# Four engines in one Mamba unit: gate and product for u later in the scan order, GpSimd's drives first, a tanh in PSUM, epsilon as a column of a product

## The chip, the cores and the metric

One core of one Trainium2 chip. The metric is the device time of one execution in microseconds (us), lower is better; a kernel's figure is the median of its runs. TensorE does the products, VectorE the scans and elementwise work that reads PSUM, ScalarE the activations, GpSimd elementwise work on SBUF, SyncE issues DMAs. In profile rows they are PE (PEld for its weight loads), DVE, ACT, POOL and SP.

## The reference

Six blocks in a row on a batch of two images of 16 x 16 positions and 64 channels: triangular edge attention, attention with rotary embedding, attention with 8 heads of 64, a top-2 mixture of 8 experts, a stack of six Mamba layers and a second mixture of experts, with normalisations and residuals. The change concerns the Mamba stack alone:

```python
for i in range(6):
    residual = hidden if residual is None else hidden + residual
    h = residual * rsqrt(mean(residual ** 2) + 1e-5) * norm_w[i]
    u, z = split(h @ in_w[i])                       # 128 channels each, 256 positions
    uc = silu(causal_conv(u, cw[i]) + cb[i])        # 4 taps
    dt_r, Bm, Cm = split(uc @ xp_w[i])              # 16, 16, 16
    dt = softplus(dt_r @ dt_w[i] + dt_b[i])
    s = exp(dt[..., None] * A) * s + (dt * uc)[..., None] * Bm      # scanned over 256 positions
    y = sum(s * Cm) + uc * Dp
    hidden = (y * silu(z)) @ out_w[i]
```

## The kernel before, in words

The kernel is written by hand, engine by engine: each engine's block is a fixed list of instructions in program order, and semaphores alone tie the engines together. No scheduler reorders anything: what stands behind a waiting instruction on its engine waits too.

The Mamba stack is 12 **units**, u = 2 * layer + image (`UNITS`). A unit holds channels on 128 partitions and 256 positions (N) along the free axis; its 16 states are four groups g = 0 to 3 of four (`SG`), so one scan runs over 4 x 256 = 1024 columns. The two images alternate, so that unit u+1 is prepared while u is scanned; unit u+1 of the same image as u-1 needs u-1's output. In one turn of the loop over u:

- **VectorE**: `prep_dt(u)` (three products on 256 columns: L1151 finishes the softplus polynomial, L1154 makes `dt`, L1157 makes `dtu` = dt * uc), `drive(u,0)` (L1170, dtu times the spread B of group 0), `gate(u-1)` (L1163, y of the unit before times its gz), four `scan`s (L1179), `drive(u,1)`, `prep_uc(u+1)` (L1145) and `weigh_last` (L1189, group 3 times C in two halves).
- **GpSimd**: `drive(u,2)` and `drive(u,3)` (L1689), `prep_rms(u+1)` (L1672 adds epsilon, L1674 takes the power -0.5), six halves of `weigh` for groups 0 to 2 (L1700, scanned states times C, 512 columns each) and `prep_gz` (L1680, z times its sigmoid).
- **ScalarE**: sixteen `decay`s (L1484, exp(dt * A) into PSUM, four per scan; `da` has two buffers, so those of group g+2 wait for scan g), and u+1's preparation: square and sum (`prep_norm`, L1414), scaling (`prep_hs`, L1428), `ht` (L1434), tanh for silu(u) (`prep_tu`, L1440), the copy of z (`prep_zs`, L1445), `xds` and `stack` (L1458, L1459), the softplus steps (L1468 to L1474), and z's sigmoid (L1451, L1453).
- **TensorE**: `out_proj(u-1)` after the gate (L708, L711, its sum with the residual stays in PSUM as `hidp`), the spreads of B and C (`replicate`, L664), for u+1 the transposes, the convolution (`prep_in`, L633 to L635), z's product (L640) and `prep_x`, and `sum_y` (L698): sixteen products with the identity that add up y, each when its piece of `hc` is there. The last one raises `m_y`.
- **SyncE** stores `xds` and reads it back spread over all partitions: groups 2 and 3 of B, 0 to 2 of C, five loads of 512 KB per unit.

The chain from one unit to the unit after next runs through all engines: gate(u-1), out_proj(u-1), prep_norm(u+1), GpSimd's prep_rms(u+1), prep_hs, transposes, ht, prep_in, tu, prep_uc(u+1), prep_x, softplus, prep_dt(u+1). The order that matters most here is GpSimd's:

```python
for u in range(UNITS):                   # GpSimd, before
    drive(u, 2)
    if u and more: prep_rms(u + 1)
    weigh(u, 0, 2)
    drive(u, 3)
    weigh(u, 1, 2); weigh(u, 2, 2)
    if more: prep_gz(u + 1)
```

## Time and profile before

| what | value |
|---|---|
| time, median of 3 runs | 377.95 us (376.48 to 378.31) |
| the profiled execution's own time | 374.24 us |
| its span, first to last instruction | 372.4 us |
| busy: PE, DVE, ACT, POOL | 88%, 78%, 63%, 54% |
| mean granted TensorE clock | 0.945 |
| the Mamba loop, first scan to last scan's start | 159.6 to 339.3 us |

The span is cut on the page into 40 slices of 9.3 us; the Mamba loop fills slices 18 to 37, where DVE's digit is 9 throughout. Busy shares over the whole span mix six blocks; the loop has to be read by itself, in order of time. A row of a timeline has start, duration, engine, line, operation, tiles and count; a bracket is idle time of the engine before it and what ended it. Instructions of one engine may overlap by some 0.08 us, so costs below are taken from start to start.

### The profile page before, as it was taken

To read this page: it belongs to the slowest core of one execution; us is meant where nothing else is said; L and a number is where in the kernel's file an instruction comes from. 1 tells how busy PE (TensorE), PEld (TensorE's weight loads), DVE (VectorE), ACT (ScalarE), POOL (GpSimd) and SP (SyncE) were. 2 spreads that over 40 slices of the span, in tenths; PEclk is the share of its full clock that TensorE was granted. 3 is DMA by queue.
4 is the path that set the end of the run, shared out by engine and by line. 5 is a ranking of instruction groups with operands and counts; after the bars stand their busy time and mean duration, and the time that the engine had idled before them with its cause. 6 is when DMAs were issued, how large, how long until landed. Compare 5 with 4: busy or idle time off the path is not lost.

```text
span 372.4 us, 5741 instructions
## 1 busy us (share of the span) xinstructions
PE 327.1 (88%) x1904; PEld 230.4 (62%) x1904; DVE 289.1 (78%) x496; ACT 235.7 (63%) x674; POOL 199.3 (54%) x199
## 2 busy tenths in 40 slices
PE   4866999899999999869999999999999999978684
PEld 3354776556557646647677676676766767656462
DVE  2674476888794626199999999999999999999463
ACT  1102348888792563777877878778787787873163
POOL 2879300000000140188978989798897988979000
PEclk9995589999999699999999999999999999998978
DMA  7960400000000030257173471734518246260000
GB/s 214 373 125 2 128 2 1 2 0 3 3 0 2 0 114 2 73 213 250 54 267 121 163 236 52 282 114 172 217 73 282 95 191 197 92 282 0 3 0 14
DMA packets 19751, 41.07 MB, mean 110 GB/s; under 512 B 7986, under 2 KB 10626, under 8 KB 19594
## 3 DMA queue, kind: packets, MB, share of 16 engines
q1 hardware_dynamic: 19434, 40.38, 31.8%
q8 instruction: 15, 0.25, 0.3%
q10 hardware_dynamic: 288, 0.33, 0.3%
q14 instruction: 14, 0.11, 0.1%
HBM read 40.31 MB, written 0.39 MB: 109 GB/s over the span
## 4 chain that ended last, share of the span: by engine, by line
PE 40%; DVE 33%; ACT 14%; POOL 5%; issue 5%; DMA 1%; POOLq 0%; DVEq 0%; SPq 0%; ACTq 0%
DVE big L1179 15%; ACT PS L1484 7%; POOL big L1700 4%; PE PS L521 4%; DVE big L1189 3%; DVE big L1151 3%; PE PS L698 3%; PE PS L297 2%; PE PS L485 2%; PE PS L640 2%; PE PS L415 2%; PE PS L585 2%; PE PS L291 2%; PE PS L495 2%; DVE unit_t L1154 1%
## 5 line engine op out<-in xcount | busy, mean ns | idle before, releaser
L1179 DVE TENSOR_TENSOR_SCAN big<-PS,big 128x1024 f32<-128x1024 f32 x48 | 109.5, 2285 | 3.0 <-ACT PS L1484 2.5
L698 PE MATMUL PS<-big,cst 128*128 128x256 f32 x384 | 98.2, 393 | 5.5 <-POOL big L1700 4.5
L1484 ACT ACTIVATE PS<-unit_t,amat 128x255 f32<-128x255 f32 x192 | 82.5, 467 | 21.3 <-DVE unit_t L1154 18.1
L1700 POOL TENSOR_TENSOR big<-big 128x512 f32<-128x512 f32 x72 | 89.4, 1268 | 2.4 <-DVE big L1179 2.2
L698 PEld LDWEIGHTS PS<-big,cst 128*128 128x128 f32 x384 | 68.2, 192 | 25.3 <-POOL big L1700 17.1
L1689 POOL TENSOR_TENSOR big<-unit_t,big 128x1024 f32<-128x1024 f32 x24 | 57.4, 2390 | 15.8 <-DMA big<-spill 15.8
L1656 POOL TENSOR_TENSOR w2t<-w2t,w0t 128x768 f32<-128x768 f32 x2 | 3.6, 1812 | 88.8 <-DVE big L1113 88.8
L1295 ACT ACTIVATE big<-PS 128x512 f32<-128x512 f32 (+1 forms) x43 | 24.7, 583 | 22.6 <-PE PS L521 7.4
L1347 ACT ACTIVATE big<-PS,big 128x256 f32<-128x256 f32 x64 | 29.6, 473 | 1.8 <-DVE big L953 1.7
L1170 DVE TENSOR_TENSOR big<-unit_t,PS 128x1024 f32<-128x1024 f32 x24 | 29.0, 1208 | 1.3
L953 DVE TENSOR_REDUCE big<-PS 128x2 f32<-128x512 f32 x32 | 22.0, 688 | 6.6 <-PE PS L415 3.2
L521 PE MATMUL PS<-cst,big 128*128 128x128 f32 x128 | 20.9, 285 | 3.2 <-ACT big L1295 1.9
L664 PE MATMUL PS<-stack,pick_b 96*128 96x256 bf16 x144 | 22.1, 276 | 1.2 <-DVE big L1170 1.2
L521 PEld LDWEIGHTS PS<-cst,big 128*128 128x128 f32 x128 | 13.5, 140 | 14.4 <-DVE big L962 6.9
L962 DVE TENSOR_SCALAR big<-big 128x256 f32<-128x256 f32 x64 | 19.7, 350 | 1.1
L664 PEld LDWEIGHTS PS<-stack,pick_b 96*128 96x128 bf16 x144 | 14.1, 99 | 7.9 <-DVE big L1170 1.6
L297 PE MATMUL PS<-cst 128*128 128x256 f32 x52 | 15.8, 442 | 0.3 <-ACT wdt L1295 0.3
L1189 DVE TENSOR_TENSOR big<-big,PS 128x512 f32<-128x512 f32 x24 | 15.4, 684 | 0.4
L1151 DVE SCALAR_TENSOR_TENSOR big<-big 128x256 f32<-128x256 f32 x12 | 10.2, 854 | 5.2 <-ACT big L1474 5.2
L1672 POOL TENSOR_TENSOR msq<-ssq,eps_t 128x2 f32<-128x2 f32 x11 | 2.1, 194 | 20.8 <-ACT sqs L1414 20.8
L1347 ACT ACTIVATION_READ_ACCUMULATOR big<-PS,big 128x1 f32 x64 | 13.2, 207 | 0.0
L1464 ACT ACTIVATE stack<-PS 96x256 bf16<-96x256 f32 x24 | 8.9, 370 | 6.2 <-PE PS L656 6.2
...
## 6 DMA issues: line engine op xcount, KB each, us to landing
...
```

Source lines behind the costliest of these rows:

```text
L297: pe.matmul(PS[:, bank, N:2 * N], ident, CONST.of(cst, "rope")[:, 0:N], start=True, stop=True)
L521: last = pe.transpose(PS[:, 6 + t, m * N + a * P:m * N + (a + 1) * P], probs[:, i % SLOTS, a, m * P:(m + 1) * P], ident)
L664: last = pe.matmul(PS[:, 4 + c, s * N:(s + 1) * N], pick_b[:, col:col + 1].to_broadcast([96, P]), stack[u % 2][:], start=True, stop=True)
L698: last = pe.matmul(yps, ident, hc[:, g, s], start=False, stop=True, skip_group_check=True)
L1170: v.tensor_tensor(dbu[:, g], dtu[u % 2].unsqueeze(1).to_broadcast([P, SG, N]), BCv, ALU.mult)\
L1179: v.tensor_tensor_scan(flat(hst[:, g]), flat(da[g % 2]), flat(dbu[:, g]), 0.0, ALU.mult, ALU.add).then_inc(sem("m_h"), 1)
L1189: v.tensor_tensor(hc[:, g, s], hst[:, g, s], BCv[:, s], ALU.mult).then_inc(sem("m_hc3"), 1)
L1295: copy = lambda dst, src, **kw: act.activation(dst, src, ACT.Copy, **kw)
L1347: act.activation(probs[:, i % SLOTS, a], PS[:, i % 4, a * N:(a + 1) * N], ACT.Exp, bias=rowmax[:, i, a:a + 1], accum_out=rowsum[:, i, a:a ...
L1484: one = act.activation(da[g % 2][:, n, 1:N], dt[u % 2][:, 1:N], ACT.Exp, scale=amat[:, u // 2, col:col + 1])
L1689: pool.tensor_tensor(dbu[:, g], dtu[b].unsqueeze(1).to_broadcast([P, SG, N]), bsp[b][:, SG * (g - 2):SG * (g - 1)], ALU.mult).then_inc(sem ...
L1700: pool.tensor_tensor(hc[:, g, s:s + size], hst[:, g, s:s + size], csp[u % 2][:, SG * g + s:SG * g + s + size], ALU.mult).then_inc(sem("m_h ...
```

## The change: what it does

In the turn of the loop for unit u:

1. **VectorE**: `gate(u-1)` moves behind `scan(u,0)`, `prep_uc(u+1)` from behind scan 1 to behind scan 2.
2. **GpSimd**: `prep_gz(u-1)` (it was gz of u+1 at the turn's end) and both drives come first, then the six halves of `weigh` in the order of `weigh_order`. `prep_rms` keeps its place behind the first drive.
3. **ScalarE**: all of group 1's decays and two of group 2's come ahead of `prep_norm`; z is copied and its sigmoid made in unit u itself, not a unit ahead; the softplus takes its exponential first, and its last tanh is written into PSUM (`outer`, free columns of `da[0]`), where L1151 (now L1156) reads it.
4. **TensorE**: the second spread comes first, then `out_proj`; z's product comes behind it, `sum_y` follows `weigh_order`.
5. **Epsilon**: a matmul adds a column sqrt(64 * 1e-5) to each half of `hidp`, ScalarE squares and sums 65 columns, and GpSimd's addition (L1672) goes, but for u = 1.

```diff
 VectorE
             v.wait_ge(sem("m_sp"), 4 * u + 4)
-            v.scalar_tensor_tensor(sp_l, sp_w, LOG_D / LOG_S, sp_u, ALU.add, ALU.mult)...
+            v.scalar_tensor_tensor(by_four(sp_l), outer, LOG_D / LOG_S, by_four(sp_u), ALU.add, ALU.mult)...
...
             for u in range(UNITS):
                 prep_dt(u)
                 drive(u, 0)
+                scan(u, 0)
                 if u:
                     gate(u - 1)
-                scan(u, 0)
                 drive(u, 1)
                 scan(u, 1)
+                scan(u, 2)
                 if u + 1 < UNITS:
                     prep_uc(u + 1)
-                scan(u, 2)
                 scan(u, 3)
                 weigh_last(u)
 GpSimd (prep_rms)
                 pool.wait_ge(sem("m_ssq"), u)
-                pool.tensor_tensor(msq[b][:], ssq[b][:], eps_t[:].to_broadcast([P, 2]), ALU.add)...
-                pool.wait_ge(sem("m_rms"), 2 * u - 1)
-                pool.tensor_tensor(rms[b][:], msq[b][:], power_t[:].to_broadcast([P, 2]), ALU.pow)...
+                mean = ssq[b]
+                if u == 1:
...
+                pool.tensor_tensor(rms[b][:], mean[:], power_t[:].to_broadcast([P, 2]), ALU.pow)...
 GpSimd (loop)
+        weigh_order = [(0, 0), (1, 0), (2, 0), (1, 1), (0, 1), (2, 1)]
             for u in range(UNITS):
+                if u:
+                    prep_gz(u - 1)
                 drive(u, 2)
-                if u and more:
+                if u and u + 1 < UNITS:
                     prep_rms(u + 1)
-                weigh(u, 0, 2)
                 drive(u, 3)
-                weigh(u, 1, 2)
-                weigh(u, 2, 2)
-                if more:
-                    prep_gz(u + 1)
+                for g, h in weigh_order:
+                    weigh(u, g, h)
+            prep_gz(UNITS - 1)
 ScalarE (prep_softplus, then the loop)
+                act.activation(sp_u, sp_a, ACT.Exp, scale=-1.0, bias=logs_t)...
+                act.activation(sp_v, sp_a, ACT.Tanh, scale=LOG_K, bias=turn_t)...
                 prep_part(u, 1)
-                act.activation(sp_w, sp_v, ACT.Tanh, scale=LOG_M, bias=shift_t)...
+                act.activation(outer, by_four(sp_v), ACT.Tanh, scale=LOG_M, bias=shift_t)...
+                prep_part(u, 2)
...
                 decay(u, 0, every)
-                decay(u, 1, every[0:2])
+                decay(u, 1, every)
+                decay(u, 2, every[0:2])
                 if u and more: prep_norm(u + 1)
+                prep_zs(u)
                 if u: keep_residual(u - 1)
-                decay(u, 1, every[2:3])
+                decay(u, 2, every[2:3])
                 if u and more: prep_hs(u + 1)
-                decay(u, 1, every[3:4])
-                decay(u, 2, every[0:1])
+                prep_zt(u)
+                decay(u, 2, every[3:4])
                 if more: prep_ht(u + 1)
-                decay(u, 2, every[1:4])
+                decay(u, 3, every[0:3])
                 if more: prep_tu(u + 1)
...
+                prep_zc(u)
                 decay(u, 3, every[3:4])
                 if more: prep_softplus(u + 1)
 TensorE
+                spread_second(u)
                 if u:
                     out_proj(u - 1)
+                prep_in_z(u)
+                spread_last(u)
...
+                sum_y(u, 3, (1, 2))
+                sum_y(u, 0, (2, 3))
+                sum_y(u, 1, (3,))
+                sum_y(u, 3, (3,))
+                sum_y(u, 2, (2, 3)).then_inc(sem("m_y"), 1)
```

GpSimd, one turn of the loop for an odd unit. `ssq` and `rms` carry the image's number; unit_t holds uc, gz, dt, dtu, z, and big the drives, states and weighed states. Before:

```order
L1689 TENSOR_TENSOR big<-unit_t,big 128x1024 [waits m_h,m_dtu,ld_B12]
L1672 TENSOR_TENSOR msq0<-ssq0,eps_t 128x2 [waits m_ssq]
L1674 TENSOR_TENSOR rms0<-msq0,power_t 128x2 [waits m_rms]
L1700 TENSOR_TENSOR big<-big 128x512 [waits m_y,m_h,ld_C10]
L1700 TENSOR_TENSOR big<-big 128x512
L1689 TENSOR_TENSOR big<-unit_t,big 128x1024 [waits m_h,m_dtu,ld_B13]
L1700 TENSOR_TENSOR big<-big 128x512 [waits m_y,m_h,ld_C11]
L1700 TENSOR_TENSOR big<-big 128x512
L1700 TENSOR_TENSOR big<-big 128x512 [waits m_y,m_h,ld_C12]
L1700 TENSOR_TENSOR big<-big 128x512
L1680 TENSOR_TENSOR unit_t<-unit_t 128x256 [waits m_zt]
```

The same turn in the changed kernel:

```order
L1684 TENSOR_TENSOR unit_t<-unit_t 128x256 [waits m_zt]
L1693 TENSOR_TENSOR big<-unit_t,big 128x1024 [waits m_h,m_dtu,ld_B12]
L1678 TENSOR_TENSOR rms0<-ssq0,power_t 128x2 [waits m_ssq]
L1693 TENSOR_TENSOR big<-unit_t,big 128x1024 [waits m_h,m_dtu,ld_B13]
L1703 TENSOR_TENSOR big<-big 128x512 [waits m_y,m_h,ld_C10]
L1703 TENSOR_TENSOR big<-big 128x512 [waits m_y,m_h,ld_C11]
L1703 TENSOR_TENSOR big<-big 128x512 [waits m_y,m_h,ld_C12]
L1703 TENSOR_TENSOR big<-big 128x512 [waits m_y,m_h,ld_C11]
L1703 TENSOR_TENSOR big<-big 128x512 [waits m_y,m_h,ld_C10]
L1703 TENSOR_TENSOR big<-big 128x512 [waits m_y,m_h,ld_C12]
```

Behind the power of `ssq` stand the same drive and six weighs as before, with the drive now ahead of the first two weighs and without the addition ahead of the power; gz, of the unit before, has moved from the end to the head of the turn.

VectorE, from `prep_dt(u)` to the last scan, in the same turn. Before:

```order
L1151 SCALAR_TENSOR_TENSOR big<-big 128x256 [waits m_sp]
L1154 SCALAR_TENSOR_TENSOR unit_t<-PS,big 128x256 [waits m_xs,m_poly]
L1157 SCALAR_TENSOR_TENSOR unit_t<-unit_t 128x256 [waits m_uc,m_dt]
L1170 TENSOR_TENSOR big<-unit_t,PS 128x1024 [waits m_dtu,m_BC]
L1163 TENSOR_TENSOR unit_t<-PS,unit_t 128x256 [waits m_gz,m_y]
L1179 SCALAR_TENSOR_TENSOR big<-PS,big 128x1024 [waits m_hc,m_da,m_dbu]
L1170 TENSOR_TENSOR big<-unit_t,PS 128x1024 [waits m_BC]
L1179 SCALAR_TENSOR_TENSOR big<-PS,big 128x1024 [waits m_hc,m_da,m_dbu]
L1145 SCALAR_TENSOR_TENSOR unit_t<-unit_t,PS 128x256 [waits m_tu]
L1179 SCALAR_TENSOR_TENSOR big<-PS,big 128x1024 [waits m_hc,m_da,m_dbu_pool]
L1179 SCALAR_TENSOR_TENSOR big<-PS,big 128x1024 [waits m_da,m_dbu_pool]
```

In the changed kernel:

```order
L1156 SCALAR_TENSOR_TENSOR big<-PS,big 128x256 [waits m_sp]
L1160 SCALAR_TENSOR_TENSOR unit_t<-PS,big 128x256 [waits m_xs,m_poly]
L1163 SCALAR_TENSOR_TENSOR unit_t<-unit_t 128x256 [waits m_uc,m_dt]
L1176 TENSOR_TENSOR big<-unit_t,PS 128x1024 [waits m_dtu,m_BC]
L1185 SCALAR_TENSOR_TENSOR big<-PS,big 128x1024 [waits m_hc,m_da,m_dbu]
L1169 TENSOR_TENSOR unit_t<-PS,unit_t 128x256 [waits m_gz,m_y]
L1176 TENSOR_TENSOR big<-unit_t,PS 128x1024 [waits m_BC]
L1185 SCALAR_TENSOR_TENSOR big<-PS,big 128x1024 [waits m_hc,m_da,m_dbu]
L1185 SCALAR_TENSOR_TENSOR big<-PS,big 128x1024 [waits m_hc,m_da,m_dbu_pool]
L1150 SCALAR_TENSOR_TENSOR unit_t<-unit_t,PS 128x256 [waits m_tu]
L1185 SCALAR_TENSOR_TENSOR big<-PS,big 128x1024 [waits m_hc,m_da,m_dbu_pool]
```

The gate has moved one scan back and the product for u one scan back; the first of the three small products now has an operand in PSUM, the third (dt * uc) still has both in SBUF.

## Rows read from the trace of the kernel before

**Rows 1.** Busy time by stretch, the loop and the last unit's middle (length, PE, PEld, DVE, ACT, POOL, clock, DMA).

```profile
190.00:206.00 16.00, 15.11 (x82) 11.23 (x80) 15.38 (x14) 12.59 (x38) 14.09 (x12) 1.00 0.52 181
...
333.00:337.00 4.00, 1.99 (x9) 1.19 (x7) 3.97 (x3) 2.06 (x6) 3.06 (x3) 0.77 0.14 58
```

**Rows 2.** Timeline of VectorE over one unit (start, duration, engine, line, operation, tiles, count).

```profile
187.46 0.89 DVE L1151 SCALAR_TENSOR_TENSOR big<-big 128x256 f32<-128x256 f32 x1
188.38 0.42 DVE L1154 SCALAR_TENSOR_TENSOR unit_t<-PS,big 128x256 f32<-128x256 f32 x1
188.84 0.42 DVE L1157 SCALAR_TENSOR_TENSOR unit_t<-unit_t 128x256 f32<-128x256 f32 x1
189.37 1.22 DVE L1170 TENSOR_TENSOR big<-unit_t,PS 128x1024 f32<-128x1024 f32 x1
190.50 0.42 DVE L1163 TENSOR_TENSOR unit_t<-PS,unit_t 128x256 f32<-128x256 f32 x1
190.84 2.28 DVE L1179 TENSOR_TENSOR_SCAN big<-PS,big 128x1024 f32<-128x1024 f32 x1
193.04 1.20 DVE L1170 TENSOR_TENSOR big<-unit_t,PS 128x1024 f32<-128x1024 f32 x1
194.27 2.29 DVE L1179 TENSOR_TENSOR_SCAN big<-PS,big 128x1024 f32<-128x1024 f32 x1
196.71 0.42 DVE L1145 SCALAR_TENSOR_TENSOR unit_t<-unit_t,PS 128x256 f32<-128x256 f32 x1
...
199.56 2.29 DVE L1179 TENSOR_TENSOR_SCAN big<-PS,big 128x1024 f32<-128x1024 f32 x1 [0.23 <-ACT PS L1484]
201.88 1.29 DVE L1189 TENSOR_TENSOR big<-big,PS 128x512 f32<-128x512 f32 x2
203.08 0.90 DVE L1151 SCALAR_TENSOR_TENSOR big<-big 128x256 f32<-128x256 f32 x1
```

**Rows 3.** One line's instructions: L1151 and L1210 of VectorE (ns min/median/max, first and last start).

```profile
L1151 DVE SCALAR_TENSOR_TENSOR big<-big x12: 425/892/903, 156.2 to 328.1; 128x256 f32<-128x256 f32 x12
...
L1210 DVE TENSOR_TENSOR Z<-Y x2: 292/636/979, 342.8 to 348.2; 128x128 f32<-128x128 f32 x2
```

**Rows 4.** Timeline of GpSimd over the same unit.

```profile
189.40 2.40 POOL L1689 TENSOR_TENSOR big<-unit_t,big 128x1024 f32<-128x1024 f32 x1 [1.33 <-DMA big<-spill]
192.27 0.19 POOL L1672 TENSOR_TENSOR msq<-ssq,eps_t 128x2 f32<-128x2 f32 x1 [0.47 <-ACT sqs L1414]
192.54 0.69 POOL L1674 TENSOR_TENSOR rms<-msq,power_t 128x2 f32<-128x2 f32 x1
193.25 2.50 POOL L1700 TENSOR_TENSOR big<-big 128x512 f32<-128x512 f32 x2
195.71 2.39 POOL L1689 TENSOR_TENSOR big<-unit_t,big 128x1024 f32<-128x1024 f32 x1
198.05 4.96 POOL L1700 TENSOR_TENSOR big<-big 128x512 f32<-128x512 f32 x4
202.97 0.73 POOL L1680 TENSOR_TENSOR unit_t<-unit_t 128x256 f32<-128x256 f32 x1
```

**Rows 5.** Timeline of GpSimd, its last instructions in the Mamba stack.

```profile
338.73 4.95 POOL L1700 TENSOR_TENSOR big<-big 128x512 f32<-128x512 f32 x4
```

**Rows 6.** Timeline of ScalarE over the same unit, the steps that prepare the next one.

```profile
191.67 0.22 ACT L1414 ACTIVATE sqs<-PS 128x64 f32<-128x64 f32 x1 [0.37 <-PE PS L711]
...
193.26 0.52 ACT L1428 ACTIVATE hs<-PS,rms 128x64 f32<-128x64 f32 x2 [0.54 <-POOL rms L1674]
...
194.54 0.47 ACT L1434 ACTIVATE ht<-PS,cols 128x256 f32<-128x256 f32 x1
...
196.29 0.38 ACT L1440 ACTIVATE unit_t<-PS 128x256 f32<-128x256 f32 x1
...
198.98 0.47 ACT L1484 ACTIVATE PS<-unit_t,amat 128x255 f32<-128x255 f32 x1
```

**Rows 7.** Timeline of TensorE ahead of the first unit: z's product, then a filler.

```profile
150.01 0.70 PE L640 MATMUL PS<-ht,inz 64*128 64x256 f32 x2
150.64 0.48 PE L723 MATMUL PS<-cst 128*128 128x256 f32 x1
```

More of the change, by code:

```diff
@@ L214, in hybrid @@
         BCv = PS[:, 4:6].rearrange("p c (s n) -> p (c s) n", n=N)
+        weigh_order = [(0, 0), (1, 0), (2, 0), (1, 1), (0, 1), (2, 1)]
+        outer = da[0][:, :, 1:1 + N // SG]
+        by_four = lambda t: t.rearrange("p (s n) -> p s n", s=SG)
         yps, zps = PS[:, 6, 0:N], PS[:, 6, N:2 * N]
         ups, xd, dtp = PS[:, 7, 0:N], PS[0:96, 7, 0:N], PS[:, 7, N:2 * N]
-        hidp = PS[:, 7, 0:P].rearrange("p (a c) -> p a c", a=HALF)
+        hidden = PS[:, 7, 0:HALF * (D + 1)].rearrange("p (a c) -> p a c", a=HALF)
+        hidp, eps_col = hidden[:, :, 0:D], hidden[:, :, D:D + 1].rearrange("p a c -> p (a c)")
+        root_eps = sb("root_eps", [P, HALF])
         def pair_of(bank, c):
@@ L639, in prep_in_z @@
                 i, b = divmod(u, 2)
-                pe.matmul(zps, inz[:, i], ht[b][0:64, 3:3 + N], start=(u == 0), stop=True, skip_group_check=True)\
-                    .then_inc(sem("m_in"), 1)
+                pe.wait_ge(sem("m_gate"), u)
+                pe.matmul(zps, inz[:, i], ht[b][0:64, 3:3 + N], start=True, stop=True).then_inc(sem("m_inz"), 1)
             def prep_x(u):
@@ L708, in out_proj @@
                 pe.matmul(hidp, ident, Y[:, :, b], start=True, stop=False)
+                pe.matmul(eps_col, ident, root_eps[:], start=False, stop=False)
                 pe.wait_ge(sem("m_gate"), u + 1)
@@ L1413, in prep_norm @@
                 for a in range(HALF):
-                    last = act.activation(sqs[:, a], hidp[:, a] if u >= 2 else Y[:, a, b], ACT.Square, scale=D ** -0.5,
+                    src = hidden[:, a] if u >= 2 else Y[:, a, b]
+                    last = act.activation(sqs[:, a, 0:D + (u >= 2)], src, ACT.Square, scale=D ** -0.5,
                                           accum_out=ssq[b][:, a:a + 1])
@@ L1508, in _ @@
                     prep_norm(u + 1)
+                prep_zs(u)
                 if u:
                     keep_residual(u - 1)
-                decay(u, 1, every[2:3])
+                decay(u, 2, every[2:3])
                 if u and more:
                     prep_hs(u + 1)
-                decay(u, 1, every[3:4])
-                decay(u, 2, every[0:1])
+                prep_zt(u)
+                decay(u, 2, every[3:4])
                 if more:
                     prep_ht(u + 1)
-                decay(u, 2, every[1:4])
+                decay(u, 3, every[0:3])
                 if more:
                     prep_tu(u + 1)
-                decay(u, 3, every[0:1])
-                if more:
-                    prep_zs(u + 1)
-                decay(u, 3, every[1:3])
-                if more:
-                    prep_xd(u + 1)
+                prep_zc(u)
                 decay(u, 3, every[3:4])
@@ L1671, in prep_rms @@
                 pool.wait_ge(sem("m_ssq"), u)
-                pool.tensor_tensor(msq[b][:], ssq[b][:], eps_t[:].to_broadcast([P, 2]), ALU.add).then_inc(sem("m_rms"), 1)
-                pool.wait_ge(sem("m_rms"), 2 * u - 1)
-                pool.tensor_tensor(rms[b][:], msq[b][:], power_t[:].to_broadcast([P, 2]), ALU.pow).then_inc(sem("m_rms"), 1)
+                mean = ssq[b]
+                if u == 1:
+                    pool.tensor_tensor(msq[b][:], ssq[b][:], eps_t[:].to_broadcast([P, 2]), ALU.add).then_inc(sem("m_rms"), 1)
+                    pool.wait_ge(sem("m_rms"), 1)
+                    mean = msq[b]
+                pool.tensor_tensor(rms[b][:], mean[:], power_t[:].to_broadcast([P, 2]), ALU.pow).then_inc(sem("m_rms"), 1)
             def prep_gz(u):
@@ L1690, in drive, with weigh @@
                                    bsp[b][:, SG * (g - 2):SG * (g - 1)], ALU.mult).then_inc(sem("m_dbu_pool"), 1)
-            def weigh(u, g, parts=1):
+            def weigh(u, g, h):
                 pool.wait_ge(sem(f"ld_C{u % 2}{g}"), 16 * (u // 2 + 1))
@@ L1697, in weigh @@
                     pool.wait_ge(sem("m_y"), u)
-                for n in range(parts):
-                    s, size = SG // parts * n, SG // parts
-                    pool.tensor_tensor(hc[:, g, s:s + size], hst[:, g, s:s + size],
-                                       csp[u % 2][:, SG * g + s:SG * g + s + size], ALU.mult).then_inc(sem("m_hc"), 1)
+                t = slice(2 * h, 2 * h + 2)
+                pool.tensor_tensor(hc[:, g, t], hst[:, g, t], csp[u % 2][:, SG * g + 2 * h:SG * g + 2 * h + 2], ALU.mult)\
+                    .then_inc(sem("m_hc"), 1)
             prep_rms(1)
-            prep_gz(0)
             for u in range(UNITS):
-                more = u + 1 < UNITS
+                if u:
+                    prep_gz(u - 1)
                 drive(u, 2)
-                if u and more:
+                if u and u + 1 < UNITS:
                     prep_rms(u + 1)
-                weigh(u, 0, 2)
                 drive(u, 3)
-                weigh(u, 1, 2)
-                weigh(u, 2, 2)
-                if more:
-                    prep_gz(u + 1)
+                for g, h in weigh_order:
+                    weigh(u, g, h)
+            prep_gz(UNITS - 1)
 def constants():
```

78 lines of the change are left out of this document (33 added, 45 removed).

## The prediction, as put on record before the changed kernel ran

> **What bounds the kernel now.** The page's digits put the Mamba loop first: half of the span, VectorE at 9 throughout. By stretch, 16 us of it hold 15.38 us of VectorE, 14.09 of GpSimd, 15.11 of TensorE and 12.59 of ScalarE, at a granted clock of 1.00, the full 2.4 GHz [rows 1]. VectorE's timeline shows why it leads: from one L1151 to the next it runs with one idle gap of 0.23 us, and the unit takes 203.08 - 187.46 = 15.62 us [rows 2]. GpSimd sits close behind: it ends a unit at 202.97 + 0.73 = 203.70, when VectorE is already in the next [rows 2, 4]. So VectorE's own time sets the unit now, and GpSimd's order is the first that could take its place.
>
> One row in VectorE's list is out of line. L1151 takes 0.89 us, its neighbours on equally many columns take 0.42 [rows 2]; it took 0.425 once, its minimum [rows 3]. L1151 at 203.08 has both operands in SBUF, and GpSimd's gz product is running, 202.97 to 203.70 [rows 4]. It ends at 203.98, so if it works 0.42 us it begins at 203.56, 0.14 ahead of gz's end. The same is seen against a weigh: L1210, also two operands in SBUF, takes 0.979 instead of 0.292 [rows 3]. It starts at 342.84 and ends at 343.82, so it begins its 0.29 at 343.53, while the last weigh of four ends at 338.73 + 4.95 = 343.68 [rows 5], 0.15 later. VectorE's products with one operand in PSUM pay nothing: L1145 takes 0.42 at 196.71, inside a GpSimd drive that runs from 195.71 to 198.10 [rows 2, 4]. I read this as: a VectorE instruction with two SBUF operands stands still until the GpSimd instruction under way is within 0.14 us of its end.
>
> **The change, part by part.**
>
> *Tanh into PSUM.* L1151 gets an operand in PSUM and should take 0.42: it gives 0.92 - 0.46 = 0.46 us a unit (187.46 to 188.38 against 188.38 to 188.84). The tanh itself is one ScalarE instruction as before, and ScalarE has 3.4 us of 16 to spare [rows 1].
>
> *Epsilon in the product.* GpSimd's L1672 goes, 192.54 - 192.27 = 0.27 us. The added two-column product stands ahead of TensorE's wait for the gate, and the squares grow by one column of 64: nothing on the path.
>
> *Gate and product for u one scan later.* Neither costs VectorE time. But the whole chain to u+1 hangs on the gate, and so does GpSimd: the power of `ssq` waits for it, and the second drive and all six weighs queue behind the power. Write G for a gate's start. Before, the power's predecessor starts at 192.27 - 190.50 = G + 1.77 [rows 2, 4]; the way there (out_proj, squares from G + 1.17, [rows 6]) is unchanged. So in the new order, with spacings from [rows 4]: power at G + 1.77; second drive 0.71 later (192.54 to 193.25); first weigh 2.34 later (195.71 to 198.05); the last weigh five spacings of 1.23 later (four take 198.05 to 202.97). The last weigh starts at **G + 10.97** and, 1.27 long, stops blocking at 10.97 + 1.27 - 0.14 = **G + 12.10**.
>
> VectorE from the same gate, by start-to-start times of [rows 2]: drive 0.34, scan 1 after 1.23, scan 2 after 2.20, G + 3.77 if its decays are there. ScalarE has the last of them at: power's end 2.46, scaling 2.49 + 0.52, z's tanh 0.38, a decay 0.47 [rows 6], about G + 3.9. The product for u follows at 3.9 + 2.20 = 6.1. Scan 3 waits for its last decay: scaling to `ht` 1.28, `ht` to tu 1.75, then tu, z's copy and a decay, 0.38 + 0.38 + 0.47 [rows 6], with 0.1 for the hand-over: G + 6.85, where VectorE alone would be free at 6.44. Then 2.32 to the weigh of group 3, 1.20 to the polynomial, 0.46 and 0.46 to dt * uc: **G + 11.29**.
>
> dt * uc has both operands in SBUF. Before, it ran in GpSimd's idle time (188.84 to 189.26; GpSimd idle for 1.33 us until 189.40) and took 0.42. Now it comes 0.32 us after the last weigh has begun, and stands until G + 12.10. The wait that L1151 loses is taken up, larger, by L1157's successor. From there 0.53 to the drive (188.84 to 189.37), 1.23 to the scan, 2.20 to the next gate: 12.10 + 3.96 = **16.06 us a unit against 15.62, +0.44**. This loop runs over GpSimd, so VectorE's own savings no longer count, nor would a VectorE delay of up to 0.8 us (a late softplus, say). Between the eleven gates inside the loop there are ten such units: +4.4.
>
> The Trainium skill (SBUF — State Buffer, Who interferes with whom) speaks against the change here: it says that a VectorE instruction with two SBUF inputs and a GpSimd instruction that reads SBUF lock each other out for the full instruction. The rows agree on who waits and differ on when it ends, 0.14 us early; by the skill's rule dt * uc would start at G + 12.24, the unit would take 16.20, and the sum below would end 1.4 us higher, at 382.8.
>
> *z later, drives first, the order of weighs.* Moving the second drive ahead of two weighs changes no GpSimd sum. gz moves to GpSimd's head, behind the last weigh; the gate needs it only 4 us later. The loads from `spill` start with `xds`, hence with the product for u, at G + 6.1; in the unit shown the first was there within 8.3 us of that product (196.71 to the next drive, one unit after 189.40), so at G + 14.4, and the first drive ends by G + 16.8, ahead of the next power at G + 17.8: hidden. z's product ahead of the first unit goes (150.01 to 150.64, [rows 7]): -0.6.
>
> *Ends.* Unit 0 has no gate and no power, its weighs follow the scans at once, and dt * uc meets the last weigh's end: VectorE's own chain, some 14.7 instead of 15.6: -0.9. The first gate comes one scan later (+2.5), the last unit gives that back (-2.5); there GpSimd's last four weighs wait for the third scan, 1.7 us behind VectorE's end instead of 343.68 - 342.84 = 0.84, with fewer sums behind them: +0.5.
>
> Sum: -0.6 - 0.9 + 2.5 + 4.4 - 2.5 + 0.5 = **+3.4 us**. Against the profiled execution, 374.24 us (span 372.4 and 1.84 around), that is 377.6; the median of the runs shown, 377.95, is 1% above that execution, and the difference carried over gives **381.4 us**. Unknown costs: when the blocked instruction begins (0.14 early or at the end: 0 to +1.4), unit 0 (±0.3), TensorE's share in the way from gate to squares (±0.05 a unit, ±0.5): 380 to 384.
>
> **The rivals.**
>
> *Faster: dt * uc gets in ahead of the last weigh.* If VectorE is there before G + 10.97, it passes in the gap after the fifth weigh. It takes 0.32 us: without the waits of scan 2 and scan 3 for decays (0.13 and 0.41 above) dt * uc would come at G + 10.75. For it: these waits are sums of seven ScalarE and TensorE steps. Against: the softplus has to be done too, and any lateness of it moves the product deeper under the weigh. Then the unit takes 11.29 + 3.96 = 15.25 or less: -3.7 for ten, in sum -4.7, **373.2 us**. Chance 0.18.
>
> *gz also passes ahead.* GpSimd's next instruction after the last weigh is gz, 0.73 us, ready at once. If the port goes to it instead of the waiting VectorE, each unit grows by 0.73: +7.3, **388.7 us**. Nothing in the rows has two GpSimd instructions in a queue ahead of a waiting product, but L1151 and L1210 began 0.14 before the other's end, ahead of any next start. Chance 0.05.
>
> *The tanh in PSUM doesn't help.* L1151's successor at G + 10.37 would stand under the fifth weigh until 10.87 and push the last weigh back by up to 0.42: some +0.3 a unit more, **384.4 us**. L1145's row speaks against it. Chance 0.04.
>
> *In between:* dt * uc is caught in some units only, or GpSimd's chain is 0.3 to 0.5 shorter than summed: about **378**. Chance 0.06.
>
> **How the numbers follow.** Forecast 0.67 (380 to 384), faster rival 0.18, the others 0.05, 0.04 and 0.06. A measurement of this kernel tells about 0.5%, 1.9 us, from no change. Faster is the first rival and a sliver of the last, 0.19; within 0.5% most of the last and the low edge of the forecast, 0.07; slower the rest, 0.74. The likeliest case alone reaches from 380 to 384; to leave out no more than 2 in 10 the range has to reach down to the faster rival: 372.8 to 384.5.
>
> **What would show it.** Right: L1156 near 0.42 us; L1163 (dt * uc) near 1.2, ending some 0.3 us behind the last weigh in every unit but the first; a loop of about 16.1 us from scan to scan; GpSimd idle only ahead of the power. Wrong: L1163 at 0.42 with a loop near 15.2 (the faster rival), L1163 near 1.9 with gz ahead of it, L1156 near 0.9, or a granted clock below 1.00 inside the loop, as in the one thin stretch of before, 0.77 with TensorE busy 1.99 of 4 us [rows 1].

## The result and the profile after the change

| | before | after |
|---|---|---|
| time, median of 4 runs each | 377.22 us (374.21 to 378.31) | 385.20 us (383.02 to 386.04) |
| ratio | 1 | 1.0228 (interval 1.0179 to 1.0276) |
| profiled execution, its span | 374.24, 372.4 us | 385.42, 383.6 us |
| first scan of the stack, its last unit's first scan | 159.59, 331.52 us | 160.68, 340.93 us |

The changed kernel is 8.0 us slower, where +3.4 was forecast, with a time of 381.4 and a range up to 384.5. The direction was right, the size was not. (Ratios below leave disturbed runs out; medians are over all runs of a kernel.)

VectorE's timeline of a unit after the change, which answers to [rows 2] (columns as there):

```profile
189.95 0.42 DVE L1156 SCALAR_TENSOR_TENSOR big<-PS,big 128x256 f32<-128x256 f32 x1
190.40 0.42 DVE L1160 SCALAR_TENSOR_TENSOR unit_t<-PS,big 128x256 f32<-128x256 f32 x1
190.85 1.24 DVE L1163 SCALAR_TENSOR_TENSOR unit_t<-unit_t 128x256 f32<-128x256 f32 x1
192.20 1.22 DVE L1176 TENSOR_TENSOR big<-unit_t,PS 128x1024 f32<-128x1024 f32 x1
193.45 2.29 DVE L1185 TENSOR_TENSOR_SCAN big<-PS,big 128x1024 f32<-128x1024 f32 x1
195.66 0.40 DVE L1169 TENSOR_TENSOR unit_t<-PS,unit_t 128x256 f32<-128x256 f32 x1
...
201.75 0.40 DVE L1150 SCALAR_TENSOR_TENSOR unit_t<-unit_t,PS 128x256 f32<-128x256 f32 x1
202.42 2.29 DVE L1185 TENSOR_TENSOR_SCAN big<-PS,big 128x1024 f32<-128x1024 f32 x1 [0.27 <-ACT PS L1493]
...
205.95 0.42 DVE L1156 SCALAR_TENSOR_TENSOR big<-PS,big 128x256 f32<-128x256 f32 x1
```

The polynomial (L1156) has fallen from 0.89 to 0.42 us, as forecast. dt * uc (L1163) has risen from 0.42 to 1.24, as forecast too. From one L1156 to the next it is 205.95 - 189.95 = 16.00 us, against 15.62 before and 16.06 forecast. GpSimd's timeline over the same stretch, which answers to [rows 4]:

```profile
188.08 3.73 POOL L1703 TENSOR_TENSOR big<-big 128x512 f32<-128x512 f32 x3
191.78 0.91 POOL L1684 TENSOR_TENSOR unit_t<-unit_t 128x256 f32<-128x256 f32 x1
193.65 2.35 POOL L1693 TENSOR_TENSOR big<-unit_t,big 128x1024 f32<-128x1024 f32 x1 [0.97 <-DMA big<-spill]
197.41 0.69 POOL L1678 TENSOR_TENSOR rms<-ssq,power_t 128x2 f32<-128x2 f32 x1 [1.41 <-ACT sqs L1421]
198.06 2.41 POOL L1693 TENSOR_TENSOR big<-unit_t,big 128x1024 f32<-128x1024 f32 x1
200.38 7.46 POOL L1703 TENSOR_TENSOR big<-big 128x512 f32<-128x512 f32 x6
207.76 0.77 POOL L1684 TENSOR_TENSOR unit_t<-unit_t 128x256 f32<-128x256 f32 x1
```

The last weigh ends at 188.08 + 3.73 = 191.81. dt * uc ends at 192.09, so its 0.42 us of work began at 191.67, 0.14 ahead of that end. The Trainium skill (SBUF — State Buffer, Who interferes with whom) gives the lock for the whole instruction; here too the release comes 0.14 us ahead of the weigh's recorded end, and the unit takes 16.00 us, not the 16.20 worked out from that rule.

So far this is the forecast. The next unit is not:

```profile
206.86 1.95 DVE L1163 SCALAR_TENSOR_TENSOR unit_t<-unit_t 128x256 f32<-128x256 f32 x1
...
219.31 0.42 DVE L1150 SCALAR_TENSOR_TENSOR unit_t<-unit_t,PS 128x256 f32<-128x256 f32 x1 [0.76 <-ACT unit_t L1447]
```

These are VectorE's rows one and two turns on. Here dt * uc takes 1.95 us: it ends at 208.81, 0.28 behind **gz** (L1684, 207.76 to 208.53 in GpSimd's rows above). gz, queued behind the last weigh, went ahead of the waiting product. Then the product for u (L1150) stands 0.76 us for a tanh of ScalarE's that is late. Busy time by stretch shows why (length, PE, PEld, DVE, ACT, POOL, granted clock, DMA share, GB/s), beside [rows 1]:

```profile
162.00:178.00 16.00, 13.79 (x61) 10.33 (x62) 13.51 (x13) 10.00 (x27) 11.16 (x10) 0.79 0.34 128
190.00:206.00 16.00, 14.86 (x82) 11.12 (x81) 15.41 (x15) 12.08 (x37) 13.62 (x11) 1.00 0.50 166
206.00:222.00 16.00, 14.46 (x74) 10.90 (x73) 14.64 (x12) 10.62 (x33) 12.79 (x10) 0.89 0.48 164
238.00:254.00 16.00, 14.43 (x74) 10.56 (x73) 14.37 (x14) 10.95 (x33) 12.78 (x10) 0.89 0.47 166
302.00:318.00 16.00, 15.02 (x76) 11.28 (x74) 14.60 (x13) 11.76 (x36) 13.65 (x11) 0.89 0.48 166
```

Before the change TensorE was granted 1.00, its full 2.4 GHz, in every unit from the first to the last but one. Now it runs part of unit 0 (the first row) and part of three later units at 1.2 GHz. Its waits for the gate, in the timeline of TensorE, first before the change and then after it:

```profile
190.98 0.66 PE L711 MATMUL PS<-wout,unit_t 128*128 128x64 f32 x4 [0.39 <-DVE unit_t L1163]
```

```profile
196.11 0.66 PE L715 MATMUL PS<-wout,unit_t 128*128 128x64 f32 x4 [0.78 <-DVE unit_t L1169]
...
212.82 0.66 PE L715 MATMUL PS<-wout,unit_t 128*128 128x64 f32 x4 [1.47 <-DVE unit_t L1169]
```

It waited 0.39 us for a gate; now it waits 0.78 us, and 1.47 in the unit in which gz went ahead.

Where the 11.2 us between the two spans lie: the first scan comes 1.09 later (the blocks ahead of the stack end 2.05 later in this execution, the way from there is 0.96 shorter); unit 0 takes 16.76 in place of 15.63, +1.1; the ten units from there to the last unit's first scan take 163.49 in place of 156.30, +7.2; what follows, +1.8, of which 0.8 up to the last gate. In these ten units: ten times 0.37 for the blocked product, twice 0.71 for gz, and three times 0.69 where the clock fell. So 3.0 of the 11.2 us (2.05 ahead of the stack, 1.0 behind it) lie in blocks that the change doesn't touch; the stack itself is 8.2 longer.

### The profile page after: what moved, and what is told of

The parts are those of the page before. It is cut to its first block, busy times and chain, and to the rows that moved or that the text cites. A ratio compares the mean times of both kernels' runs of the same rounds, so it can differ in the third digit from the quotient of the medians.

```text
span 383.6 us, 5805 instructions
## 1 busy us (share of the span) xinstructions
PE 335.1 (87%) x1928; PEld 237.5 (62%) x1928; DVE 293.8 (77%) x496; ACT 234.3 (61%) x674; POOL 197.9 (52%) x190
## 4 chain that ended last, share of the span: by engine, by line
PE 46%; DVE 31%; issue 10%; ACT 9%; POOL 1%; DMA 1%; POOLq 1%; DVEq 0%; SPq 0%; ACTq 0%
DVE big L1185 8%; DVE big L1176 4%; PE PS L526 4%; DVE big L1195 4%; DVE unit_t L1163 3%; PE PS L721 3%; PE PS L627 2%; PE PS L302 2%; PE PS L490 2%; PE PS L420 2%; PE PS L590 2%; PE PS L715 2%; PE PS L296 2%; PE PS L500 2%; PE PS L727 2%
## 5 line engine op out<-in xcount | busy, mean ns | idle before, releaser
L701 PE MATMUL PS<-big,cst 128*128 128x256 f32 x384 | 92.6, 382 | 2.8 <-POOL big L1703 2.3
L701 PEld LDWEIGHTS PS<-big,cst 128*128 128x128 f32 x384 | 69.4, 190 | 15.5 <-POOL big L1703 7.3
L669 PE MATMUL PS<-stack,pick_b 96*128 96x256 bf16 x144 | 22.6, 280 | 3.5 <-DVE big L1176 3.5
L669 PEld LDWEIGHTS PS<-stack,pick_b 96*128 96x128 bf16 x144 | 13.2, 99 | 12.2 <-DVE big L1176 7.8
L721 PE MATMUL PS<-cst,zero_t 128*128 128x256 f32 x44 | 18.3, 506 | 0.0
L715 PE MATMUL PS<-wout,unit_t 128*128 128x64 f32 x48 | 7.9, 287 | 8.9 <-DVE unit_t L1169 8.9
L1678 POOL TENSOR_TENSOR rms<-ssq,power_t 128x2 f32<-128x2 f32 x10 | 6.9, 691 | 16.1 <-ACT sqs L1421 16.1
L1163 DVE SCALAR_TENSOR_TENSOR unit_t<-unit_t 128x256 f32<-128x256 f32 x12 | 13.3, 1112 | 0.4
```

Of the source, the lines that this page charges most:

```text
L669: last = pe.matmul(PS[:, 4 + c, s * N:(s + 1) * N], pick_b[:, col:col + 1].to_broadcast([96, P]), stack[u % 2][:], start=True, stop=True)
L701: last = pe.matmul(yps, ident, hc[:, g, s], start=False, stop=True, skip_group_check=True)
L721: pe.matmul(PS[:, 6, N:2 * N], zero_t[:, 0:1].to_broadcast([P, P]), CONST.of(cst, "rope")[:, 0:N], start=False, stop=True, skip_group_chec ...
L1163: v.scalar_tensor_tensor(dtu[b], dt[b], 0.5, uc[b], ALU.mult, ALU.mult).then_inc(sem("m_dtu"), 1)
```

## The experiments

Theories, as the expectations name them. **A**: dt * uc stands behind GpSimd's last weigh, or weigh and gz, and that loop sets the unit. **B**: the later gate and the chain over ScalarE and TensorE set it, and the wait is incidental. **C**: TensorE's clock falls because TensorE waits too long for what the change delays.

### What holds the unit at 16.0

**uc_in_psum**: ScalarE copies uc into free PSUM columns, and dt * uc reads it there, so it has one SBUF operand.

```diff
-v.scalar_tensor_tensor(dtu[b], dt[b], 0.5, uc[b], ALU.mult, ALU.mult)
+v.scalar_tensor_tensor(by_four(dtu[b]), by_four(dt[b]), 0.5, uc_ps, ALU.mult, ALU.mult)
...
+act.activation(uc_ps, by_four(uc[u % 2]), ACT.Copy)   # end of prep_softplus
...
+if g == 1: act.wait_ge(sem("m_dtu"), u + 1)   # in decay: group 1 overwrites these columns
```

> The changed kernel, with ScalarE copying uc into free PSUM columns behind its softplus, so that dt * uc has one operand in PSUM. Theory A (dt * uc stands behind GpSimd's last weigh, or behind gz, and that loop over GpSimd sets the unit): dt * uc takes 0.42 us in every unit instead of 0.68 to 1.95, the undisturbed unit falls from 16.00 to 15.2 to 15.3, and the time from 385.2 to 373 to 376 us, faster than before the change. Theory B (the unit is long because the gate, one scan later, starts the chain over ScalarE and TensorE later; the wait of dt * uc only fills idle time): dt * uc takes 0.42 but the unit stays near 16.0, 383 to 385 us. Theory C (the three units of 16.7 with the clock below 1.00 come from TensorE waiting long for a gate that the blocked product delays): by A's side, no such stretch is left in the loop.

Measured: 372.33 us, ratio 0.9897 (0.9839 to 0.9954). VectorE's rows:

```profile
192.60 0.40 DVE L1171 TENSOR_TENSOR unit_t<-PS,unit_t 128x256 f32<-128x256 f32 x1
...
203.80 0.42 DVE L1165 SCALAR_TENSOR_TENSOR unit_t<-unit_t,PS 128x256 f32<-128x256 f32 x1
...
207.79 0.40 DVE L1171 TENSOR_TENSOR unit_t<-PS,unit_t 128x256 f32<-128x256 f32 x1
```

dt * uc takes 0.42 while GpSimd weighs, gates lie 15.19 us apart, and behind unit 0 the loop has no half clock any more (unit 0 keeps it, granted 0.80). A holds; B, which had the wait incidental, falls.

**weigh_waits**: the same by GpSimd's order; the last weigh waits for dt * uc.

```diff
+if (g, h) == (2, 1) and u + 1 < UNITS:
+    pool.wait_ge(sem("m_dtu"), u + 2)
 weigh(u, g, h)
```

> The changed kernel with one wait more: GpSimd's last weigh of a unit waits until dt * uc of the next unit is done. Theory A: dt * uc meets only the tail of the fifth weigh and takes 0.42 to 0.5 us, the unit falls to 15.2 to 15.5, and the time to 374 to 378 us, though GpSimd does nothing sooner. Theory B: the unit stays near 16.0 or grows, since GpSimd ends later: 385 us or more.

Measured: 373.60 us, ratio 0.9926 (0.9889 to 0.9963), units of 15.19 us. GpSimd gives up 0.78 us a unit and the loop gains 0.81:

```profile
203.31 1.27 POOL L1703 TENSOR_TENSOR big<-big 128x512 f32<-128x512 f32 x1 [0.78 <-DVE unit_t L1163]
```

**tanh_only**: the kernel before, with the tanh in PSUM as the one edit.

```diff
-v.scalar_tensor_tensor(sp_l, sp_w, LOG_D / LOG_S, sp_u, ALU.add, ALU.mult)
+v.scalar_tensor_tensor(by_four(sp_l), outer, LOG_D / LOG_S, by_four(sp_u), ALU.add, ALU.mult)
...
-act.activation(sp_w, sp_v, ACT.Tanh, scale=LOG_M, bias=shift_t)
+act.activation(outer, by_four(sp_v), ACT.Tanh, scale=LOG_M, bias=shift_t)
```

> The kernel before with one part of the change alone: the softplus's last tanh is written into PSUM. Theory A: the polynomial takes 0.42 instead of 0.89 us, dt * uc stays at 0.42 because gz is over by then, the unit falls from 15.63 to 15.2, the time from 377.2 to 372 us. Theory B (ScalarE's and TensorE's preparation sets the unit): the polynomial takes 0.42 but waits for the softplus instead; the unit stays at 15.5 to 15.6 and the time at 376 to 377 us.

Measured: 376.11 us, ratio 0.9985 (0.9944 to 1.0026), no difference that can be told. VectorE's rows:

```profile
190.01 0.42 DVE L1153 SCALAR_TENSOR_TENSOR big<-PS,big 128x256 f32<-128x256 f32 x1
...
192.95 0.42 DVE L1165 TENSOR_TENSOR unit_t<-PS,unit_t 128x256 f32<-128x256 f32 x1 [0.28 <-PE PS L700]
```

The polynomial takes 0.42, but the gate, 0.46 earlier, now waits 0.28 for TensorE's last sums of the unit before. The unit is 15.52 us: of 0.46 only 0.1 arrives. In the old order the sums stand next in line. A's 372 is missed; B's unit and time came, but not by the wait for the softplus that B named.

**gate_first**: the changed kernel with the gate back ahead of the first scan.

```diff
+if u: gate(u - 1)
 scan(u, 0)
-if u: gate(u - 1)
```

> The changed kernel with the gate back ahead of the first scan, all else as changed. Theory A: the gate, and with it GpSimd's six weighs, come 2.2 us earlier against dt * uc, so that product takes 0.42; the unit falls to 15.2 to 15.7, the time to 373 to 379 us. The gate may now wait for the last sums: the last weigh ends 12.2 us behind a gate, its sums 1.4 later, so no more than 0.5 us a unit of that. Theory B also expects a shorter unit, since the chain starts earlier, but with dt * uc still meeting a weigh at some 1.2 us.

A miss: 410.72 us, ratio 1.0917 (1.0847 to 1.0988). VectorE's gate, then TensorE's second spread:

```profile
234.20 0.42 DVE L1169 TENSOR_TENSOR unit_t<-PS,unit_t 128x256 f32<-128x256 f32 x1 [2.07 <-PE PS L701]
```

```profile
237.99 0.61 PE L669 MATMUL PS<-stack,pick_b 96*128 96x256 bf16 x4 [1.92 <-DVE big L1176]
```

With all six weighs at the end of GpSimd's turn, the sums end too late for a gate that early, which waits 2.07 us. VectorE stands, TensorE then waits 1.92 us for VectorE's second drive, and its clock falls to half in a part of every unit (granted 0.82 to 0.91 over a unit). So the gate behind the first scan is what GpSimd's new order needs.

### Why it cost more than forecast: gz and the clock

**gz_behind**: gz behind GpSimd's first drive.

```diff
-if u: prep_gz(u - 1)
 drive(u, 2)
+if u: prep_gz(u - 1)
```

> The changed kernel with one step moved: gz stands behind GpSimd's first drive of the unit instead of ahead of it, so that what follows the last weigh in GpSimd's queue needs dt * uc itself and cannot pass ahead of it. A (the product for u stands behind the last weigh, or behind weigh and gz): no product of 1.95 us any more, all blocked ones at 1.23 or less, two times 0.71 us less, about -1.4 us. C (the clock falls where TensorE waits long for a delayed gate, which in the changed kernel came behind both of the units in which gz passed): two of the three stretches at half clock in the loop go as well, 0.69 us each: another -1.4, so about 382.5 us. If the clock falls for another reason, the three stretches stay and the time is about 384. Undisturbed units stay at 16.0 us.

A miss: 404.65 us, ratio 1.0799 (1.0720 to 1.0878). GpSimd's rows, then VectorE's gate:

```profile
194.04 2.35 POOL L1693 TENSOR_TENSOR big<-unit_t,big 128x1024 f32<-128x1024 f32 x1 [2.54 <-DMA big<-spill]
196.35 0.73 POOL L1684 TENSOR_TENSOR unit_t<-unit_t 128x256 f32<-128x256 f32 x1
```

```profile
197.18 0.42 DVE L1169 TENSOR_TENSOR unit_t<-PS,unit_t 128x256 f32<-128x256 f32 x1 [1.54 <-POOL unit_t L1684]
```

The first drive waits for its load, gz now waits with it, and the gate waits 1.54 us for gz (15.5 us in eleven). TensorE's own wait for the gate is then 1.33 to 2.26 us, and in nine of the ten units from unit 1 on its clock fell (granted 0.81 to 0.91). It overshot the test: what I took for a free move put a DMA on the path to the gate.

**filler**: one matmul by zeros ahead of TensorE's wait for the gate, in every unit but the last.

```diff
 pe.matmul(eps_col, ident, root_eps[:], start=False, stop=False)
+if u + 1 < UNITS:
+    pe.matmul(dtp, zero_t[:, 0:1].to_broadcast([P, P]), CONST.of(cst, "rope")[:, 0:N], start=False, stop=True, ...)
```

> The changed kernel with one matmul by zeros more per unit on TensorE (into PSUM columns that the next unit overwrites), ahead of its wait for the gate: about 0.22 us of work inside a wait of 0.78 us (1.47 us behind the units where gz passed). gz may still pass ahead. C: with the wait cut, no stretch at half clock inside the loop, three times 0.69 us less, about -2.1 us: 383; units of 16.0 us, or 16.7 where gz passes. If the clock does not depend on that wait, units of 16.7 with a half clock remain, and the time is 385.

**after_again**: the changed kernel as it is, once more.

> The changed kernel itself once more, on the chip and in the rounds of the others. Time again near 385 (ratio 1.023). If the stretches at half clock in the loop and the units in which gz passes ahead belong together, as in the first profile where two of three stretches came right behind such units, a unit with a product of 1.95 us is followed by a half clock here too; how many there are may differ. The undisturbed units take 16.0 us.

Measured: filler 381.19 us, ratio 1.0164 (1.0107 to 1.0220); the changed kernel again 388.77, ratio 1.0348 (1.0286 to 1.0410), above its first 1.0228. One line's instructions (ns min/median/max), dt * uc in filler and in the changed kernel again:

```profile
L1165 DVE SCALAR_TENSOR_TENSOR unit_t<-unit_t x12: 424/1234/1240, 158.5 to 335.3; 128x256 f32<-128x256 f32 x12
```

```profile
L1163 DVE SCALAR_TENSOR_TENSOR unit_t<-unit_t x12: 424/1580/1968, 158.8 to 342.4; 128x256 f32<-128x256 f32 x12
```

and both loops by busy time:

```profile
178.00:338.00 160.00, 154.35 (x824) 113.80 (x823) 153.92 (x131) 121.59 (x362) 136.75 (x101) 1.00 0.47 168
```

```profile
178.00:339.00 161.00, 149.00 (x777) 111.01 (x776) 150.79 (x125) 116.80 (x350) 129.97 (x96) 0.96 0.46 162
```

In the profiled filler no gz passes, the clock is full behind unit 0, and units are 16.00 us from the third on. In the changed kernel's second profile gz passes in six of eleven, units of 16.7 are the rule, and all three falls of the clock behind unit 0 come where gz has just passed (the longest of these units is 17.69 us). But filler changed two things at once: its matmul shortened TensorE's wait, and gz happened not to pass.

**gz_waits**: gz keeps its place, but needs dt * uc of the same unit, so that it can't go ahead of it.

```diff
 if u:
+    pool.wait_ge(sem("m_dtu"), u + 1)
     prep_gz(u - 1)
```

> The changed kernel with gz in its place, but waiting for dt * uc of the same unit, so that it can't start ahead of it; the first drive of GpSimd behind it needs dt * uc too, and its load came 2.06 us after dt * uc (gz_behind: 191.98 to 194.04), so gz's 0.73 us are hidden there. If gz ahead of the waiting product is what was missing in the size: no product of 1.95, all units 16.0 us, no half clock inside the loop or one at most, and a ratio of 1.012 to 1.016, as filler had without such units, against 1.023 and 1.035 of the changed kernel. If the half clock has another cause, units of 16.7 with a wait of the product for u remain and the ratio stays above 1.02.

Measured: 380.83 us, ratio 1.0104 (1.0058 to 1.0149), clear of the changed kernel's two intervals. dt * uc in its trace, and gz in GpSimd's:

```profile
L1163 DVE SCALAR_TENSOR_TENSOR unit_t<-unit_t x12: 424/1226/1266, 155.4 to 332.3; 128x256 f32<-128x256 f32 x12
```

```profile
188.73 0.73 POOL L1684 TENSOR_TENSOR unit_t<-unit_t 128x256 f32<-128x256 f32 x1 [0.36 <-DVE unit_t L1163]
190.16 2.35 POOL L1693 TENSOR_TENSOR big<-unit_t,big 128x1024 f32<-128x1024 f32 x1 [0.70 <-DMA big<-spill]
```

No product above 1.27 us, eight of ten units of 16.0, and gz is done 0.70 us before the load that the drive needs: it costs nothing there. That gz ahead of the product, with the longer wait of TensorE that follows from it, is what was missing in the size is thereby shown; this run does not tell the two apart. Two units still ran partly at half clock (16.59 and 16.28 us), with no gz ahead of anything, so passing is not the only cause of the falls.

**gz_waits_filler**: gz_waits, filler's matmul, and matmuls in unit 0 (next section).

> The changed kernel with gz waiting for dt * uc, the matmuls in the first unit, and the matmul by zeros in each unit ahead of TensorE's wait for the gate. C: no stretch at half clock between the first and the last unit, ten units of 16.0 us, 1.3 us less than gz_waits_awake3 (16.38, 16.63 and 16.31 become 16.0): about 379.0, ratio 1.005 to 1.007. If the clock falls for another reason: two or three units above 16.2 and a ratio of 1.009.

Measured: 379.63 us, ratio 1.0046 (1.0005 to 1.0087). The loop by busy time, the same of gz_waits_awake3, which lacks only the matmul by zeros, and TensorE's wait for the gate in gz_waits_filler:

```profile
177.00:337.00 160.00, 154.36 (x824) 113.75 (x824) 153.86 (x130) 121.44 (x362) 135.07 (x100) 1.00 0.49 167
```

```profile
174.00:335.00 161.00, 153.17 (x804) 114.54 (x804) 151.75 (x130) 121.45 (x362) 135.21 (x101) 0.97 0.48 167
```

```profile
260.00 0.66 PE L717 MATMUL PS<-wout,unit_t 128*128 128x64 f32 x4 [0.26 <-DVE unit_t L1175]
```

With 0.26 us of wait in place of 0.78 no unit of the loop loses its clock, against three in the same kernel without the matmul (gz_waits_awake3, below). In the profiles C holds for the loop. In time the two kernels' intervals overlap, so its worth, 1 to 2 us, is not settled.

The profiles of the changed kernel and all its versions, seventeen with ten units each (the first and the last unit left out), say more than one pair. Of 119 units in which TensorE's longest wait was 0.64 us or less, none lost the clock; of 24 with 0.77 to 0.95 us, nine did; of 27 with 1.33 to 2.26 us, 24 did. So the longer wait makes the fall likelier, and of the seven units in which gz passed without a filler (1.47 to 1.49 us) five lost it.

### The first unit

Around the first scan TensorE waits 1.01, 1.31 and 2.20 us in the changed kernel, the longest ahead of the next unit's transposes; before it was 1.11, 1.19 and 1.72, the longest behind them. TensorE's row behind the longest wait, before and after:

```profile
163.35 0.70 PE L698 MATMUL PS<-big,cst 128*128 128x256 f32 x2 [1.72 <-POOL big L1700]
```

```profile
164.14 1.04 PE L669 MATMUL PS<-stack,pick_b 96*128 96x256 bf16 x4 [2.20 <-DVE big L1176]
```

The third spread (L669), which the change puts ahead of the transposes, waits there for VectorE's second drive, which stands behind the first scan, and in unit 0 TensorE has nothing else to do. Three tries filled them with matmuls into PSUM columns not in use.

```diff
 prep_x(0)
+keep_awake(n1)                # awake 0, awake2 4, awake3 2
 take_away(0, 0)
...
 spread_first(0)
+keep_awake(n2, 6)             # awake 0, awake2 6, awake3 2
...
 prep_in_z(u)
+if u == 0: keep_awake(n3, 7)  # awake 8 (they wait for dt too), awake2 9, awake3 4
 spread_last(u)
```

> The changed kernel with u's copy read from PSUM (372.3 us) and, in unit 0 alone, eight matmuls of TensorE into PSUM columns not in use, in the 2.20 us in which it waits for VectorE's second drive. C: the clock stays at full in unit 0, the wait of 2.0 us of the product for u behind it goes, unit 0 takes 15.2 instead of 16.9: -1.7 us, 370.6. If the fall in unit 0 has another cause, the time stays at 372.3 (+-0.3).

> The changed kernel with GpSimd's last weigh held back for dt * uc (373.6 us) and the same eight matmuls in unit 0. C: unit 0 takes about 15.2 instead of 15.7, -0.5 us, and where other executions of that kernel lost more in unit 0, more: 372 to 373. Otherwise 373.6.

Misses: ratios 0.9882 (0.9782 to 0.9982) and 0.9932 (0.9883 to 0.9980), as without the matmuls. In the profile of uc_in_psum_awake the eight took 5.41 us, far more than the 2.20 us of the wait, and the clock fell all the same.

> The changed kernel with u's copy read from PSUM (372.3 us), and in the first unit TensorE kept at work in all the stretches before the fall: four matmuls in the wait of 1.01 us ahead of the first correction of the stack, six in the wait of 1.31 us ahead of the second spread, nine in the 2.20 us ahead of the last spread. The eight matmuls in the last wait alone did not help, the clock fell 0.9 us after they had begun. If the fall comes from the thin work before 160.8 us: no stretch at half clock in unit 0, its length 15.2 instead of 16.9 us, -1.7 us: about 370.6 us (ratio 0.983 to 0.985). If unit 0's clock falls for something else: 372.3 (ratio 0.99).

> The changed kernel with GpSimd's last weigh held back for dt * uc, and the same matmuls in the first unit. As above: unit 0 in 15.2 us and 371 to 372 us if the thin work before 160.8 us is the cause, 373.6 otherwise.

> The changed kernel with one matmul by zeros ahead of the gate's wait in each unit (381.2 us, ratio 1.016), and the same matmuls in the first unit. With the clock at full through the whole loop this is the changed kernel as the prediction priced it, blocked dt * uc and all: ten units of 16.0 us, and a first unit of about 15.2 in place of 16.2: 380 (ratio 1.012). If the first unit keeps its half clock: 381.2.

Misses again: 0.9924 (0.9881 to 0.9966), 0.9946 (0.9906 to 0.9986) and 1.0250 (1.0177 to 1.0323). In filler_awake2 gz passed in six units, which alone spoils the comparison; TensorE then waited 0.93 to 0.95 us for the gate in spite of the filler, and in three of the six the clock fell. For the first unit, TensorE's rows in weigh_waits_awake2:

```profile
160.88 4.15 PE L727 MATMUL PS<-cst 128*128 128x256 f32 x18
164.87 0.60 PE L669 MATMUL PS<-stack,pick_b 96*128 96x256 bf16 x4
```

The nine matmuls are 18 passes and took 4.15 us, 0.46 each, twice what I had counted. The clock stayed full, but the last spread came 164.87 - 158.59 = 6.28 us behind the first scan's start, against 164.14 - 160.68 = 3.46 in the changed kernel, with all that queues behind it, and unit 0 still took 17.05 us. So two, two and four:

> u's copy read from PSUM and the same matmuls in the first unit. Loop of 15.19 us a unit; first unit 15.2 to 15.5 with full clock, in place of 16.9: about 1.5 us below the kernel without them, ratio 0.984 to 0.988. If the first unit keeps its length: 0.99.

> GpSimd's last weigh held back for dt * uc and the same matmuls. Loop of 15.19, first unit 15.2 to 15.5: ratio 0.985 to 0.99; 0.993 if the first unit keeps its length.

> The same, and in the first unit two, two and four matmuls of 0.46 us in TensorE's waits of 1.01, 1.31 and 2.20 us. If the half clock alone makes the first unit long (16.8 in place of about 15.2): another -1.5 us, ratio 1.008 to 1.012, which is the +3.4 us of the prediction. If the first unit is long for VectorE's wait of 1.23 for the second spread alone: some -0.5.

Measured: **370.66 us, ratio 0.9825** (0.9779 to 0.9870); 370.92, ratio 0.9828 (0.9787 to 0.9870); and 380.41, ratio 1.0092 (1.0059 to 1.0126). TensorE's rows and the first unit by busy time, in uc_in_psum_awake3:

```profile
158.67 1.99 PE L728 MATMUL PS<-cst 128*128 128x256 f32 x8
160.94 0.61 PE L670 MATMUL PS<-stack,pick_b 96*128 96x256 bf16 x4 [0.27 <-DVE big L1182]
```

```profile
157.00:172.00 15.00, 13.69 (x73) 10.01 (x73) 14.63 (x13) 10.64 (x30) 12.87 (x9) 1.00 0.48 164
```

The matmuls now fit into the waits, the clock is 1.00, and unit 0 takes 14.56 us in place of 16.88. Which of the three fillings keeps the clock is not told apart. These two are the fastest versions here, below both kernels. gz_waits_awake3 is the changed kernel as the prediction had priced it: unit 0 in 14.65 us, no gz ahead. It gained nothing that can be told against gz_waits (whose unit 0, in its profile, had lost about half as much as elsewhere: 15.70), and three of its later units ran partly at half clock.

## Why the prediction was right in kind and wrong in size

- *Tanh in PSUM.* Right: 0.42 us. Alone it moves nothing (tanh_only).
- *The loop over GpSimd.* Right, nearly to the step. With the gate at G = 195.66: power at G + 1.75 (forecast 1.77), second drive at 2.40 (2.48), product for u at 6.09 (6.1), last scan at 6.76 (6.85), dt * uc at 11.20 (11.29). The unit undisturbed: 16.00 (16.06).
- *The release.* Right as read from [rows 3 to 5]: 0.14 us ahead of the weigh's end.
- *dt * uc without the block.* The faster rival's unit of 15.25 and its 373.2 us were the right price for a thing that did not happen by itself: with the block taken away it is 15.19 us, and 372.3 and 373.6, though with a first unit that still lost clock.
- *gz also passes ahead*, put at 0.05. **This is the first of two steps that failed.** I argued that the release, 0.14 ahead of a weigh's end, lies ahead of any next start. But GpSimd's instructions overlap in the record: in [rows 4] four weighs from 198.05 last 4.96, to 203.01, and gz starts at 202.97. A lead of 0.10 us decides nothing safely, and the rival should have stood as a share of units, from none to all. It was 2 and 6 of the changed kernel's units in two profiles, 0.71 us each, and with gz held back the ratio fell from 1.0228 and 1.0348 to 1.0104. That the rival's full price, 388.7, is what the second measurement of the same kernel gave (388.77) is luck: gz passed in six of eleven units there, and the clock made up the rest.
- *The first unit*, -0.9. Right for the chain (14.65 us with the clock held), wrong for the kernel: +1.1 in the profiled run, since its clock fell. The wait of 2.20 us that the change puts ahead of the transposes was in my reach: unit 0 "has no gate and no power", so TensorE has nothing else there.
- *The clock.* **The second step that failed: a term put at nothing without a reason.** The prediction named it as a sign of being wrong and gave it no price: a unit that loses it costs 0.3 to 0.7 us, once 1.7, and unit 0 one to two. The prediction summed waits of VectorE and GpSimd, and never asked what TensorE does in its new wait of 0.78 us.
- *The sum.* Of the 8.2 us by which the stack grew in the profiled pair, 3.4 were forecast. Of the other 4.8, unit 0 holds 2.0 and the three falls of the clock 2.1, gz itself 1.4; the block is 0.7 smaller than forecast. In the second profile of the changed kernel gz holds 4.3 (six times 0.71). Once gz can't pass, the kernel's ratio is 1.0104 and 1.0092, close to the forecast's 1.009. That closeness is in part luck, since two and three units at half clock are in these kernels, which the forecast had at nothing; with those gone too (gz_waits_filler) it is 1.0046 (1.0005 to 1.0087). No run takes epsilon, z's later place or the order of the weighs alone.
